# A fused two-stage convolution and attention kernel: VectorE's order within a step, the place of a small matmul on TensorE, and where input statistics stand

## The chip, the cores and the metric

The kernel runs on one core of a Trainium2 chip. The metric is the device time of one execution in microseconds (us); lower is better. A time is compared only with times of the same kind of run on the same chip.

## The reference

The input x is 32 images of 64 channels, 28 by 28, float32. Two blocks follow each other, each with a residual.

```python
x = x + relu(sum_over_4_branches(lambda * bn2(bconv3x3(relu(bn1(bconv3x3(tile(gn(x), 4), w1))), w2))) + gn(x))
g = gn(x)                                   # second block
m = resize(masks, 28 x 28)                  # bilinear, one mask per image
mid = g * m
atten = sigmoid(conv7x7([mean_c(mid), max_c(mid), m]))
out = mid * atten
x = x + relu(5 * (instance_norm(out) * in_gamma + in_beta))
```

`gn` is a group norm with 32 groups, that is pairs of channels. `bconv3x3` is a grouped 3x3 convolution of the signs of its input and of its weights. The second convolution has real-valued relu outputs in front of its sign, so that what it really reads is whether each output of the first convolution passes a threshold.

## The kernel before

**Tiles.** A tile t holds two images (2 x 64 channels on 128 partitions, 784 columns); there are 16 tiles, 0 to 15. `X` holds the tiles (later overwritten in place by X1, the result of the first block), `o` the second block's work.

**Steps.** Each engine has its program written out by hand, in order, and waits on semaphores. The main part is a loop over k = 0 to 14, one step per tile (TensorE L1342 to L1365, VectorE L1042 to L1071, ScalarE L733 to L749, GpSimd L540 to L550 with k from 1). A step works on several tiles at once, each at another stage. What one step does, with the names used below:

- TensorE, step k: `conv2(k,0)` (L1181), `conv1(k+1,0)` (L1160), `turn(k-2,0)` (L1232, transposes of the attention input), `conv2(k,1)`, at four of the steps a `group_1` (L1120), then `group_2(k-1)` (L1128: the sum over channel pairs of X1's statistics), `conv1(k+1,1)`, on even k `attention(k-3)` (L1248), `mix(k,0)` and `mix(k,1)` (L1200), `turn(k-2,1)`, `turn(k-2,2)`, `join(k+2)` (L1142).
- VectorE, step k: `split_sums(k,0)` (L867), `stats_x1(k-1)` (L776 and L781, statistics of X1), `reduce_chunks(k-2,0)` (L908, L910: the first channel maxima), `gates(k+1,0)` (L841, L844, L847), `split_sums(k,1)`, `terms1` at four of the steps, `terms2(k-1)` (L812 to L817), `gates(k+1,1)`, `finish_block(k)` (L875), `reduce_chunks(k-2,1)` and `(k-2,2)`, and `stats_x(t)` (L776, L781) for the input tiles that the dictionaries `X_END` and `X_MID` name. `X_MID`'s tiles (9, 12 and 14, at k = 4, 6, 8) stand in front of `finish_block`.
- ScalarE, step k: `round_sums2(k,0)` (L623), `move_back(k,0)` (L630), `round_sums1(k+1,0)` (L615, writes `first`), `last_relu(k-7)` (L675), the same three for the other half, `sigmoid` (L650), `sign_x` (L583), `mean_o` (L662), `normalise2(k-1)` (L642), `square_o` (L669), `pack_signs(k+2)` (L598), `relu_block(k)` (L636).
- GpSimd, iteration k: `add_x(k-1)` (L485), `attend(k-5)` (L480), `scale3(k-6)` (L492 to L498), `last_sum(k-7)` (L521), `power2(k-1)` (L457, L459), `mask_column`, `make_u(k-1)` (L465).
- SyncE issues all the large transfers in order: the inputs, then two stores of the resized masks (L362) which wait for `keep_mask_rows` (L1010), then per step mask rows (L321), attention rows (L327, L335) and outputs (L341).

**What sets the order around the change.** These waits tie the moved pieces to others:

- `gates(t,q)` waits for ScalarE's `first` of that half (`whole1`), and its results go into S, which `conv2(t,...)` reads. Its first instruction reads `first` (int16) and writes `gate0` (float16), both in SBUF: L841. `conv2(k+1,0)` waits for both halves of `gates(k+1,...)`.
- `stats_x1(t)` waits for GpSimd's `add_x(t)`. `group_2(t)` waits for `stats_x1(t)`. `terms2(t)` waits for `group_2(t)`, and `power2(t)`, `normalise2(t)` and `make_u(t)` for it in turn.
- `mix(k,hh)` waits for `split_sums(k,hh)` and for `gates(k+1,0)`. `conv1(k+1,1)` waits for `split_sums(k,0)`.
- `attention(t)` waits for the first maxima of the next tile, since they share a PSUM bank:

```python
pe.wait_ge(pooled, t * 3 + (4 if t < NT - 3 else 3))      # L1239
```

In step k that is `attention(k-3)` and `reduce_chunks(k-2,0)`.

After the loop comes a tail for the last tiles, which the change does not touch.

Of the kernel before, what the change touches and what calls it, by code (L numbers as in the profile page):

```python
# [71 lines left out]
def wait(eng, sem, count):  # L72

    if count > 0:
        eng.wait_ge(sem, count)


def has(t):
    return 0 <= t < NT


def build(nc, x, w1, w2, par, scale1, masks, band_w, cst, out):
# [8 lines left out]
    with ctx:  # L91
# [107 lines left out]
        def sums(name, first_half=0, halves=2):  # L199
            at = LOW + HALF * first_half  # L200
            return big[SLOT[name]][:, at:at + halves * HALF]

        def c1(t, q):

            return "c2_1" if t == 0 and q == 1 else f"c1_{q}"

        def inside(padded, row=0, rows=H):
            at = padded[:, PW + 1 + row * PW:PW + 1 + (row + rows - 1) * PW + W]
            return bass.AP(at.tensor, at.offset, [list(at.ap[0]), [PW, rows], [1, W]])
# [63 lines left out]
        BATCHES = [(0, 1), (1, 2), (2, 4), (4, 6), (6, 9), (9, 12), (12, 16)]  # L273
        BATCH_STEP = {2: 3, 4: 4, 7: 5, 10: 6}

        X_END = {1: (4, 5), 2: (6,), 3: (7, 8), 4: (10,), 5: (11,), 7: (13,), 9: (15,)}
        X_MID = {4: (9,), 6: (12,), 8: (14,)}

        def batch(t):
            return next(n for n, (a, z) in enumerate(BATCHES) if a <= t < z)  # L280
# [20 lines left out]
        def turned_at(t, n):  # L301
            return LAST_BANKS[t][n] if t in LAST_BANKS else small[1 - n % 2]
# [470 lines left out]
        def _(dve):  # L773
            def stats_of(t, n, src):
                for i in range(2):
                    dve.bn_stats(bnst[:, n, t, i, :], src[:, HALF * i:HALF * (i + 1)]).then_inc(stats[n], 1)  # L776
                add_up(t, n)
# [5 lines left out]
            def stats_x(t):  # L783
                if has(t):
                    dve.wait_ge(x_in[t], 16)
                    stats_of(t, 0, X[:, t, :])

            def stats_x1(t):
                if has(t):
                    dve.wait_ge(x1_ready, t + 1)  # L790
                    stats_of(t, 1, X[:, t, :])
# [32 lines left out]
            def terms1(n):  # L824
                dve.wait_ge(group1, n + 1)
                if n >= 3:

                    dve.wait_ge(group2, next(k for k in BATCH_STEP if BATCH_STEP[k] == n))
                group_terms(0, *BATCHES[n], group1_at(n), nm1, ve1, mean1, steps1, n + 1, var1)
# [6 lines left out]
            def gates(t, q):  # L836

                row = TOP if t == 0 else 0
                at = row * W
                dve.wait_ge(whole1, t * 2 + q + 1)  # L840
                dve.tensor_scalar(gate0[:, q, at:HW], first[:, q, at:HW], thr[:, q:q + 1], GATE, ALU.is_gt, ALU.mult)\  # L841
                   .then_inc(gated0, 1)
                ps = sums(c1(t, q))[:, at:HW]
                dve.scalar_tensor_tensor(ps, first[:, q, at:HW], -IMG, ps, ALU.mult, ALU.add).then_inc(parted1, 1)  # L844
                dve.wait_ge(parted1, t * 2 + q + 1)
                wait(dve, conv2_done, t * 2 - 2)
                dve.scalar_tensor_tensor(inside(S2[:, t % 2, q, :], row, H - row),  # L847
                                         ps.rearrange("p (h w) -> p h w", w=W), thr[:, q:q + 1],
                                         gate0[:, q, at:HW].rearrange("p (h w) -> p h w", w=W), ALU.is_gt, ALU.add)\
                   .then_inc(gated, 1)  # L850
# [12 lines left out]
            def split_sums(t, hh):  # L863
                if has(t):
                    dve.wait_ge(rounded2, t * 2 + hh + 1)
                    wait(dve, y_done, (t - 2) * 2 + hh + 1)
                    dve.scalar_tensor_tensor(RD[:, t % 2, hh, 1, :], round2[:, hh, :], BASE, sums(f"c2_{hh}"),  # L867
                                             ALU.subtract, ALU.subtract).then_inc(split, 1)
# [31 lines left out]
            def reduce_chunks(t, n):  # L900
                if not has(t):
                    return
                dve.wait_ge(turned, t * 3 + n + 1)
                wait(dve, att_done, t // 2 - 1)
                j0, nj = 3 * n, min(3, NJ - 3 * n)
                ps = turned_at(t, n)[0:CP, 0:nj * (P + 2)].rearrange("p (j m) -> p j m", m=P + 2)
                dst = [red[:, t // 2 % 2, c, 1 + j0:1 + j0 + nj, 2 * (t % 2):2 * (t % 2) + 2] for c in range(2)]
                dve.tensor_reduce(dst[1], ps[:, :, 0:P].rearrange("p j (i c) -> p j i c", i=2), AX_X, ALU.max)\  # L908
                   .then_inc(maxed, 1)
                dve.tensor_copy(dst[0], ps[:, :, P:P + 2]).then_inc(pooled, 1)  # L910
# [69 lines left out]
            def keep_mask_h():  # L980
                dve.wait_ge(mask_h, 1)
                dve.tensor_copy(mh[:, :, :].rearrange("p b h -> p (b h)"), small[0][:, 0:MB * H])\
                   .then_inc(mask_hs, 1)

            def keep_mask_hw():
                dve.wait_ge(mask_hw, 1)
                ps = small[0][0:CP, 0:MB * NJ].rearrange("p (b j) -> p b j", j=NJ)
                dve.tensor_copy(mhw[:, 1:MB + 1, :], ps).then_inc(mask_hs, 1)
                dve.tensor_copy(mhw[:, 0, :], ps[:, 0, :]).then_inc(mask_hs, 1)
                dve.tensor_copy(mhw[:, MB + 1, :], ps[:, MB - 1, :]).then_inc(mask_hs, 1)  # L990
# [16 lines left out]
            def keep_mask_rows():  # L1007
                dve.wait_ge(mask_turned, 1)
                for g in range(2):
                    dve.tensor_copy(mR[:, g, :], small[0][0:CP, CP * g:CP * (g + 1)]).then_inc(mask_rows, 1)  # L1010
# [31 lines left out]
            for k in range(NT - 1):  # L1042
                split_sums(k, 0)
                if k == 0:
                    stats_x(3)
                stats_x1(k - 1)
                if k == 1:
                    keep_mask_rows()
                reduce_chunks(k - 2, 0)
                if has(k + 1):  # L1050
                    gates(k + 1, 0)
                if k == 0:
                    keep_mask_h()
                split_sums(k, 1)
                if k == 0:
                    terms1(2)
                    keep_mask_hw()
                if k in BATCH_STEP:
                    terms1(BATCH_STEP[k])
                terms2(k - 1)  # L1060
                if has(k + 1):
                    gates(k + 1, 1)
                for t in X_MID.get(k, ()):
                    stats_x(t)
                finish_block(k)
                if k == 0:
                    mix_masks()
                reduce_chunks(k - 2, 1)
                reduce_chunks(k - 2, 2)
                for t in X_END.get(k, ()):  # L1070
                    stats_x(t)  # L1071
# [39 lines left out]
        def _(pe):  # L1111
# [38 lines left out]
            def conv1(t, q):  # L1150
                pe.wait_ge(packed, t + 1)
                if q == 0:
                    wait(pe, y_added, t - 1)
                    wait(pe, gated, 2 * t - 1)
                else:
                    wait(pe, split, 2 * t - 1)
                acc = big[SLOT[c1(t, q)]]
                for s in range(KS):
                    for hh in range(2):
                        mm = pe.matmul(acc[:, LOW + HALF * hh:LOW + HALF * (hh + 1)],  # L1160
                                       w1t[64 * hh:64 * hh + 64, q, s, :],
                                       window(RH * hh, s // 3, s % 3, E[64 * hh:64 * hh + 64, t % 2, :]),
                                       start=(s == 0), stop=(s == KS - 1))
                mm.then_inc(conv1_done, 1)
# [177 lines left out]
            for k in range(NT - 1):  # L1342
                conv2(k, 0)
                conv1(k + 1, 0)
                if k == 0:
                    resize_mask()
                    group_1(2)
                if k == 1:
                    turn_mask()
                turn(k - 2, 0)  # L1350
                conv2(k, 1)
                if k == 1:
                    pe.wait_ge(mask_rows, 2)
                if k in BATCH_STEP:
                    group_1(BATCH_STEP[k])
                group_2(k - 1)
                conv1(k + 1, 1)
                if k == 0:
                    resize_mask_w()
                attention(k - 3)  # L1360
                for hh in range(2):
                    mix(k, hh)
                turn(k - 2, 1)
                turn(k - 2, 2)
                join(k + 2)  # L1365
# [97 lines left out]
```

## Time and profile before

| what | value |
|---|---|
| median of 3 runs | 243.91 us (243.69 to 244.25) |
| profiled execution, its own time | 244.12 us |
| its span | 242.2 us |
| mean granted TensorE clock | 0.973 |
| TensorE matmul busy | 212.1 us, 88% |
| VectorE busy | 213.1 us, 88% |
| ScalarE busy | 182.8 us, 75% |
| GpSimd busy | 158.8 us, 66% |

The span runs from the first to the last instruction of the profiled execution; 1.9 us of the execution's own time lie outside it. Start times in the rows are microseconds from the start of the span. In the timeline a line gives start, duration, engine, source line, operation, output and inputs, shapes, how many instructions were merged, and in brackets the idle time of that engine in front of it with what ended it.

### The profile page before, as it was taken

What the parts mean: (1) busy time and instruction counts of PE and PEld (TensorE: products, weight loads), DVE (VectorE), ACT (ScalarE), POOL (GpSimd) and SP (SyncE); (2) the same over time, 40 slices, a digit from 0 to 9 for tenths busy, and PEclk for the clock granted to TensorE, in tenths of its full rate; (3) what the DMA queues carried; (4) which work ended last, traced back from release to release, by engine and by line L of the source; (5) the groups of instructions that cost most, each with busy time, mean ns of one, the idle gap of its engine ahead of it and who ended that gap; (6) DMA issues with size and microseconds to landing.
All of it is one profiled execution on the core that took longest, in us unless ns stands there. A gap on an engine that the chain in (4) does not pass through costs nothing.

```text
span 242.2 us, 7335 instructions
## 1 busy us (share of the span) xinstructions
PE 212.1 (88%) x2834; PEld 134.2 (55%) x2834; DVE 213.1 (88%) x520; ACT 182.8 (75%) x265; POOL 158.8 (66%) x207
## 2 busy tenths in 40 slices
PE   7789988889999889999899989998999999788800
PEld 3356554555666556665556656655565656457600
DVE  4899899799999999998999899979796979989691
ACT  3973566657696779798889989898999995860592
POOL 4548431609060755749897778897878787797883
PEclk9999999999999999999999999999999999999955
DMA  6999801510111340234121712081208120713345
GB/s 212 371 284 390 346 9 43 136 45 20 49 35 38 98 106 0 69 97 108 70 69 52 218 69 66 29 244 71 69 17 254 69 69 17 250 73 96 108 168 231
DMA packets 12122, 28.85 MB, mean 119 GB/s; under 512 B 2246, under 2 KB 3655, under 8 KB 12087
## 3 DMA queue, kind: packets, MB, share of 16 engines
q1 hardware_dynamic: 11941, 28.37, 36.4%
q8 instruction: 23, 0.38, 0.6%
q14 instruction: 12, 0.10, 0.1%
q10 hardware_dynamic: 146, 0.01, 0.0%
HBM read 21.76 MB, written 6.61 MB: 117 GB/s over the span
## 4 chain that ended last, share of the span: by engine, by line
PE 37%; DVE 31%; POOL 10%; DMA 8%; issue 8%; ACT 4%; SPq 1%; DVEq 0%; POOLq 0%; ACTq 0%
PE big L1181 10%; PE big L1160 10%; DVE bnst L776 6%; PE big L1200 5%; PE small L1232 5%; DVE big L844 4%; POOL X L485 4%; DVE RD L867 4%; DMA o<-in_w 2%; POOL o L465 2%; DMA att_b<-attention_rows 2%; PE small L1248 2%; DVE S L847 2%; DVE gate L841 2%; DVE acc L875 2%
## 5 line engine op out<-in xcount | busy, mean ns | idle before, releaser
L1181 PE MATMUL big<-S,w2t 64*64 64x392 f16 x1152 | 55.3, 332 | 2.9 <-DVE S L847 2.8
L1160 PE MATMUL big<-E,w1t 64*128 64x392 f16 x576 | 54.5, 331 | 1.6 <-DVE w1t L959 0.9
L1181 PEld LDWEIGHTS big<-S,w2t 64*64 64x64 f16 x1152 | 30.8, 106 | 22.6 <-DVE S L847 7.4
L623 ACT ACTIVATE round<-big 128x784 f16<-128x784 f32 x32 | 26.1, 816 | 18.1 <-PE big L1181 17.8
L1200 PE MATMUL big<-RD,wa 128*64 128x392 f16 x384 | 35.1, 331 | 4.8 <-issue 4.8
L1160 PEld LDWEIGHTS big<-E,w1t 64*128 64x128 f16 x576 | 25.8, 94 | 23.7 <-ACT E L598 3.2
L867 DVE SCALAR_TENSOR_TENSOR RD<-round,big 128x784 f16<-128x784 f16 x32 | 30.7, 959 | 8.2 <-ACT round L623 7.9
L465 POOL TENSOR_TENSOR o<-o,mask_b 128x784 f32<-128x784 f32 x15 | 27.8, 1856 | 13.9 <-ACT o L642 10.9
L776 DVE BATCH_NORM_STATS2 bnst<-X 128x6 f32<-128x392 f32 x62 | 31.9, 556 | 3.9 <-POOL X L485 3.6
L485 POOL TENSOR_TENSOR X<-X,acc 128x784 f32<-128x784 f32 x15 | 27.7, 1849 | 10.3 <-ACT acc L636 10.1
L847 DVE SCALAR_TENSOR_TENSOR S<-big,thr,gate 128x784 f16<-128x784 f32 (+1 forms) x32 | 32.3, 1010 | 1.1
L457 POOL TENSOR_TENSOR r<-ve,mhalf 128x1 f32<-128x1 f32 x16 | 10.4, 650 | 33.0 <-DVE ve L817 32.8
L1232 PE MATMUL small<-cs,o 128*112 128x130 f32 x204 | 30.2, 288 | 1.9 <-DVE ve L817 1.4
L1200 PEld LDWEIGHTS big<-RD,wa 128*64 128x64 bf16 x384 | 22.7, 110 | 15.1 <-issue 7.9
L844 DVE SCALAR_TENSOR_TENSOR big<-first,big 128x784 f32<-128x784 int16 (+1 forms) x32 | 30.2, 945 | 0.0
L1232 PEld LDWEIGHTS small<-cs,o 128*112 128x112 f32 x204 | 24.1, 177 | 11.0 <-issue 7.4
L480 POOL TENSOR_TENSOR o<-o,att_b 128x784 f32<-128x784 f32 x14 | 25.9, 1851 | 3.7 <-DMA att_b<-attention_rows 3.7
L615 ACT ACTIVATE first<-big 128x784 int16<-128x784 f32 x30 | 24.5, 817 | 4.9 <-PE big L1160 4.9
L630 ACT ACTIVATE RD<-round 128x784 f16<-128x784 f16 x32 | 27.4, 857 | 1.0
L521 POOL TENSOR_TENSOR o<-o,X 128x784 f32<-128x784 f32 x12 | 22.1, 1844 | 0.0
L642 ACT ACTIVATE o<-X,nmr,r 128x784 f32<-128x784 f32 x15 | 15.6, 1037 | 7.0 <-POOL nmr L459 7.0
L908 DVE TENSOR_REDUCE red<-small 112x6 f32<-112x384 f32 (+1 forms) x44 | 19.4, 446 | 0.5 <-PE small L1232 0.5
(161 smaller groups left out, 326.3 us busy)
## 6 DMA issues: line engine op xcount, KB each, us to landing
X<-in_x SPq DMA_DIRECT2D x16, 392.0 KB, 13.1
mask_b<-mask_rows SPq DMA_DIRECT2D x32, 196.0 KB, 4.0
out<-o SPq DMA_DIRECT2D x15, 392.0 KB, 2.7
att_b<-attention_rows SPq DMA_DIRECT2D x28, 196.0 KB, 3.9
o<-in_w SPq DMA_DIRECT2D x3, 576.0 KB, 6.8
o<-in_masks SPq DMA_DIRECT2D x1, 512.0 KB, 9.7
band<-in_band SPq DMA_DIRECT2D x1, 441.0 KB, 10.1
cs<-in_cst SPq DMA_DIRECT2D x1, 399.0 KB, 8.8
```

Of the source, the lines that this page charges most:

```text
L465: pool.tensor_tensor(o[:, t, :], o[:, t, :], mask_b[:, t % 2, :], ALU.mult).then_inc(u_ready, 1)
L485: pool.tensor_tensor(X[:, t, :], X[:, t, :], acc0[:, t % 2, :], ALU.add).then_inc(x1_ready, 1)
L623: act.activation(round2[:, hh, :], sums(f"c2_{hh}"), ACT.Copy, bias=BASE - MID).then_inc(rounded2, 1)
L630: act.activation(RD[:, t % 2, hh, 0, :], round2[:, hh, :], ACT.Copy, bias=-BASE).then_inc(whole2, 1)
L776: dve.bn_stats(bnst[:, n, t, i, :], src[:, HALF * i:HALF * (i + 1)]).then_inc(stats[n], 1)
L844: dve.scalar_tensor_tensor(ps, first[:, q, at:HW], -IMG, ps, ALU.mult, ALU.add).then_inc(parted1, 1)
L847: dve.scalar_tensor_tensor(inside(S2[:, t % 2, q, :], row, H - row), ps.rearrange("p (h w) -> p h w", w=W), thr[:, q:q + 1], gate0[:, q, a ...
L867: dve.scalar_tensor_tensor(RD[:, t % 2, hh, 1, :], round2[:, hh, :], BASE, sums(f"c2_{hh}"), ALU.subtract, ALU.subtract).then_inc(split, 1)
L1160: mm = pe.matmul(acc[:, LOW + HALF * hh:LOW + HALF * (hh + 1)], w1t[64 * hh:64 * hh + 64, q, s, :], window(RH * hh, s // 3, s % 3, E[64 * ...
L1181: mm = pe.matmul(acc[64 * q:64 * q + 64, LOW + HALF * r:LOW + HALF * (r + 1)], w2t[64 * r:64 * r + 64, s, 64 * q:64 * q + 64], window(RH * ...
L1200: mm = pe.matmul(big[SLOT["y"]][64 * i:64 * i + 64, at:at + HALF], wa[:, i, r, n, :], RD[:, t % 2, hh, i, HALF * r:HALF * (r + 1)], start= ...
L1232: mm = pe.matmul(turned_at(t, n)[0:CP, at:at + P + 2], o[:, t, CP * j:CP * (j + 1)], turn_w[:, :] if t == LAST else cs[:, K_ID:K_ID + P + ...
```

## The change

On VectorE the step's order becomes `split_sums(k,0)`, `keep_mask_rows` (at k = 1), `gates(k+1,0)`, `stats_x1(k-1)`, `reduce_chunks(k-2,0)`, and then as before. The input statistics of tiles 9, 12 and 14 move from in front of `finish_block` to the end of the same step. On TensorE `conv1(k+1,1)` goes in front of `group_1` and `group_2(k-1)`. No instruction is added or taken away.

```diff
-        X_END = {1: (4, 5), 2: (6,), 3: (7, 8), 4: (10,), 5: (11,), 7: (13,), 9: (15,)}
-        X_MID = {4: (9,), 6: (12,), 8: (14,)}
+        X_END = {1: (4, 5), 2: (6,), 3: (7, 8), 4: (9, 10), 5: (11,), 6: (12,), 7: (13,), 8: (14,), 9: (15,)}
@@ VectorE's loop
                 split_sums(k, 0)
                 if k == 0:
                     stats_x(3)
-                stats_x1(k - 1)
                 if k == 1:
                     keep_mask_rows()
-                reduce_chunks(k - 2, 0)
                 if has(k + 1):
                     gates(k + 1, 0)
+                stats_x1(k - 1)
+                reduce_chunks(k - 2, 0)
                 if k == 0:
                     keep_mask_h()
                 split_sums(k, 1)
@@
                     gates(k + 1, 1)
-                for t in X_MID.get(k, ()):
-                    stats_x(t)
                 finish_block(k)
@@ TensorE's loop
                 if k == 1:
                     pe.wait_ge(mask_rows, 2)
+                conv1(k + 1, 1)
                 if k in BATCH_STEP:
                     group_1(BATCH_STEP[k])
                 group_2(k - 1)
-                conv1(k + 1, 1)
                 if k == 0:
                     resize_mask_w()
```

## Rows read from the trace of the kernel before

**Rows 1.** The page: busy time of each engine, and the chain that ended last, by engine.

```profile
PE 212.1 (88%) x2834; PEld 134.2 (55%) x2834; DVE 213.1 (88%) x520; ACT 182.8 (75%) x265; POOL 158.8 (66%) x207
...
PE 37%; DVE 31%; POOL 10%; DMA 8%; issue 8%; ACT 4%; SPq 1%; DVEq 0%; POOLq 0%; ACTq 0%
```

**Rows 2.** Busy time by stretch: stretch, length, PE, PEld, DVE, ACT, POOL, clock, DMA.

```profile
132.00:205.00 73.00, 70.83 (x1014) 44.99 (x1005) 63.96 (x143) 64.66 (x93) 59.91 (x70) 1.00 0.33 102
```

**Rows 3.** Timeline, step 9 and the beginning of step 10, all engines.

```profile
134.47 1.84 POOL L485 TENSOR_TENSOR X<-X,acc 128x784 f32<-128x784 f32 x1 [1.21 <-ACT acc L636]
...
135.14 0.97 DVE L867 SCALAR_TENSOR_TENSOR RD<-round,big 128x784 f16<-128x784 f16 x1 [0.92 <-ACT round L623]
...
135.90 0.81 ACT L615 ACTIVATE first<-big 128x784 int16<-128x784 f32 x1
...
136.28 1.85 POOL L480 TENSOR_TENSOR o<-o,att_b 128x784 f32<-128x784 f32 x1
136.35 1.04 DVE L776 BATCH_NORM_STATS2 bnst<-X 128x6 f32<-128x392 f32 x2 [0.24 <-POOL X L485]
...
138.04 0.42 DVE L841 TENSOR_SCALAR gate<-first,thr 128x784 f16<-128x784 int16 x1
138.10 0.41 POOL L492 TENSOR_SCALAR ve<-o_square 128x1 f32<-128x1 f32 x1
138.37 0.97 DVE L844 SCALAR_TENSOR_TENSOR big<-first,big 128x784 f32<-128x784 int16 x1
...
139.74 0.82 ACT L615 ACTIVATE first<-big 128x784 int16<-128x784 f32 x1 [0.26 <-PE big L1160]
...
140.33 0.96 DVE L867 SCALAR_TENSOR_TENSOR RD<-round,big 128x784 f16<-128x784 f16 x1
...
141.52 0.22 DVE L817 SCALAR_TENSOR_TENSOR ve<-dm,veps 128x1 f32<-128x1 f32 x1
...
143.00 1.04 DVE L847 SCALAR_TENSOR_TENSOR S<-big,thr,gate 128x784 f16<-128x784 f32 x1
...
144.09 1.33 PEld L1181 LDWEIGHTS big<-S,w2t 64*64 64x64 f16 x36 [0.39 <-DVE S L847]
...
147.04 0.97 DVE L867 SCALAR_TENSOR_TENSOR RD<-round,big 128x784 f16<-128x784 f16 x1
```

**Rows 4.** Timeline, step 10: its attention, and the start of step 11.

```profile
152.05 1.08 PE L1248 MATMUL small<-band,red 112*28 112x56 f32 x36
...
156.61 1.72 PE L1181 MATMUL big<-S,w2t 64*64 64x392 f16 x36
...
159.70 0.97 DVE L867 SCALAR_TENSOR_TENSOR RD<-round,big 128x784 f16<-128x784 f16 x1 [1.41 <-ACT round L623]
```

**Rows 5.** Timeline, conv2(k,0) of k = 5 and of k = 15, first and last of 11.

```profile
81.41 1.72 PE L1181 MATMUL big<-S,w2t 64*64 64x392 f16 x36 [0.47 <-DVE S L847]
...
204.81 1.38 PE L1181 MATMUL big<-S,w2t 64*64 64x392 f16 x28
```

**Rows 6.** Timeline, an early VectorE operation alone and beside GpSimd's add_x.

```profile
31.91 0.19 DVE L1000 TENSOR_SCALAR mlo<-mhw 112x56 f32<-112x56 f32 x1
...
32.18 1.88 POOL L485 TENSOR_TENSOR X<-X,acc 128x784 f32<-128x784 f32 x1 [3.25 <-ACT acc L636]
32.40 1.72 DVE L1000 TENSOR_SCALAR mlo<-mhw 112x56 f32<-112x56 f32 x1
```

**Rows 7.** Timeline, tile 0's short gates; then line L841 over the whole span.

```profile
16.83 0.30 DVE L841 TENSOR_SCALAR gate<-first,thr 128x364 f16<-128x364 int16 x1
17.05 0.53 DVE L844 SCALAR_TENSOR_TENSOR big<-first,big 128x364 f32<-128x364 int16 x1
...
L841 DVE TENSOR_SCALAR gate<-first,thr x32: 304/416/422, 16.8 to 202.4; 128x784 f16<-128x784 int16 x30, 128x364 f16<-128x364 int16 x2
```

**Rows 8.** Timeline, step 1's mask rows and step 2's statistics of X1.

```profile
36.48 0.40 DVE L1010 COPY mR<-small 112x112 f32<-112x112 f32 x2
...
48.36 1.04 DVE L776 BATCH_NORM_STATS2 bnst<-X 128x6 f32<-128x392 f32 x2 [1.46 <-POOL X L485]
```

## The prediction

> **What bounds the kernel now.** I read the page first, then the busy time by stretch, then the timeline of two steps in the middle. No engine alone is the bound: TensorE and VectorE are both busy 88% of the span, and the chain that ended last goes 37% through TensorE and 31% through VectorE [rows 1]. In the late steps TensorE is busy 70.8 of 73 us at the full clock, VectorE 64.0, ScalarE 64.7 [rows 2]. Ten steps, k = 5 to 14, take 204.81 - 81.41 = 123.4 us [rows 5], 12.3 each.
>
> What closes the loop of a step is seen in [rows 3], counted from the start of split_sums(k,0), called Z here (135.14). ScalarE's round ends and lets it go; behind it ScalarE needs until Z+1.6 (135.90 + 0.81 = 136.71) for `first` of the next tile. GpSimd's add_x starts at Z-0.67 and ends at Z+1.2; attend follows at once and runs from Z+1.14 to Z+2.99 (136.28 + 1.85 = 138.13). VectorE's statistics of X1 start when add_x ends, at Z+1.21, after a wait of 0.24. The first gates start at Z+2.90 (138.04), the second split at Z+5.19 (140.33), terms2 gives its variance at Z+6.4, the second gates end at Z+8.90 (144.04), and conv2 of the next step starts at 144.09, held by them. From terms2 the chain also runs through GpSimd's power and ScalarE's normalise, square, pack and relu to the next Z: 147.04, 11.90 after the last one. On even steps attention starts at Z+5.01 (152.05 against 147.04); from there TensorE is full to the next conv2(k,0), 4.56 later, and ScalarE's queue behind the sigmoid gives the next Z 7.65 after attention's start (159.70) [rows 3, 4].
>
> **The change, part by part.** No instruction is new, so the sum is made of waits.
>
> *Gates in front of X1's statistics, the main term.* In the new order the first gates could start when `first` is there, at Z+1.6. At that moment GpSimd is inside attend, from Z+1.14 to Z+2.99, in every step from k = 5 on. The question is whether L841 can run beside it. [Rows 6] show a case: L1000, a tensor_scalar with input and output in SBUF, takes 0.19 us alone, and 1.72 us when it is issued at 32.40 while add_x runs from 32.18 to 34.06; it ends at 34.12, 0.06 after add_x. So it stood still until GpSimd was done. L841 is of the same kind. It is also fast: with 364 columns the next instruction follows 0.22 us later, with 784 columns 0.33 us later (138.04 to 138.37, the next gate instruction), so 420 more columns cost 0.11 us, near four a cycle of a pass that costs L844 0.44 us for the same 420. None of its 32 instances ever took more than 0.422 us [rows 7], but all of them start where no long GpSimd operation is running: in [rows 3] it starts 0.09 us before attend's end, because the statistics and the maxima in front of it happen to take as long as attend. And GpSimd's one-element L492 beside it takes 0.41 us [rows 3]. So I bound the price of the overlap from both sides: 0 (it runs, Z+1.6) and the rest of attend, 1.35 us (Z+2.95 or so). I take the second, since the one overlap in this trace cost all of it.
>
> The Trainium skill, "SBUF — State Buffer", section "SBUF: two separate sides", says that VectorE in its two-port modes and GpSimd share one pair of ports, and that the one that starts first holds it for its whole instruction while the other blocks. By that rule the gates wait for attend; the trace agrees with it in the 1.72 us of [rows 6], and the other end of the bound would be the sum without it.
>
> Then, on odd steps: gates start at Z+2.95, their three instructions hold VectorE 2.29 us (138.04 to 140.33), statistics and maxima 1.69 (136.35 to 138.04), so the second split starts at Z+6.93 instead of Z+5.19. Everything behind hangs on it (terms2, the second gates, conv2, the next Z): +1.74. Five such steps, k = 5, 7, 9, 11, 13: +8.7.
>
> On even steps attention must wait for the maxima, which now come last. They end at Z+2.95+2.29+1.19+0.57 = Z+7.0 (1.19 for the statistics, 0.57 for the reduction with its copy), so attention starts at Z+7.05 instead of Z+5.01: +2.04, and up to +2.2 where no group_1 stood in front of it. Five such steps: +10.5. Together +19.2.
>
> *The small sum behind conv1(k+1,1).* TensorE comes to it earlier by 0.35 us and the wait of some 0.3 in front of it, and conv1 with them. That is gain only if the statistics are there when TensorE arrives. They are ready at Z+2.95+2.29+1.28 = Z+6.5, and TensorE gets there at about Z+4.2 (conv1(k+1,1) ends at about 139.7 now, when ScalarE's 139.74 can start [rows 3], and comes 0.35 or more earlier), so it stands 2 us and more. The earlier conv1 gives an earlier `first`, whose reader, the second gates, is not the last to come. Cost and gain 0; the cover of that is the statistics' wait already counted. If the gates did not have to wait, this wait would still be near 1.
>
> *The early steps.* At k = 1 the mask rows are kept before the statistics, whose 1.1 us stand in front of 36.48 now. SyncE's two stores, the mask loads behind them, and make_u(0) follow, so that add_x(1), for which VectorE waits 1.46 us at 48.36 [rows 8], ends 1.0 earlier. The DMAs keep their order on SyncE's queue and pass nothing. Until k = 4 GpSimd has no attend, and VectorE is late enough that `first` is there: the gates cost no wait. Stepped through with the durations above, conv2(3,0) comes 1.2 us earlier, steps 3 and 4 give 0.8 back through the maxima in front of attention(1), and conv2(5,0) starts 0.35 earlier. The bounds here are -1.5 and +0.5.
>
> *Input statistics at the end of the step.* Same number, three steps. finish_block(k) and with it relu and add_x come 1.2 us earlier; at k = 4 and 8 that removes ScalarE's wait, some 0.4 us each, which at k = 8 lies behind attention anyway. At k = 5, where VectorE has two tiles to do, the step also grows less, by 1.1 instead of 1.74. Together -0.6.
>
> *Sum.* 19.2 - 0.35 - 0.6 = +18.2 us at conv2(15,0). The tail starts from attention(11) and the last add_x as before, both moved with it, so I add nothing. The profiled execution took 244.12 us, so 262.3; the median of the runs shown lies 0.2 below that execution, so **262.0 us**.
>
> **The rivals.**
>
> *A, the gates run beside attend.* For it: L1000 is float32 and L841 int16 to float16, and only one case is in the trace. Against: the kind of operands is the same. Then the gates start at Z+1.6: +0.4 on odd steps, and attention at Z+5.7, +0.7 to +0.9 on even ones. 5 x 0.4 + 5 x 0.8 = 6.0, less the early 0.35 and about 0.9 for the earlier relu in steps 5, 7 and 9: +4.8, **248.7 us**. TensorE's stop at group_2 would be seen here too.
>
> *B, the phases slip.* The longer steps move GpSimd against VectorE. Where attend waits for its attention rows or make_u ends late, the gates come first, hold the ports for 0.33 us, and only then attend starts. If half of the ten steps fall so, half of 13.4 is saved: **255 us**.
>
> *C, the other sign.* The mask rows' gain of 1.2 us stays, and the order helps: the 0.24 us wait for add_x is gone, mix(k,0) no longer waits for the gates (it does in [rows 3]'s step until 138.04 + 2.38 = 140.42), and conv1 is not behind the sum, 0.35 us in each of five odd steps. That gives -1.2 - 1.75, **241 us**. It decides in this case only if the statistics end before TensorE comes to the sum, that is if the gates start 0.5 us or more in front of Z+1.6. ScalarE's two instructions between Z and `first` (1.6 us in [rows 3]) speak against it: they are the same in the new order.
>
> *D, nothing moves.* The early gain and the waits cancel within 0.2%, 0.5 us, which is about what a measurement of this kernel can tell from no change: **243.9 us**.
>
> **How the numbers follow.** The forecast 0.65, B 0.12, A 0.13, C 0.06, D 0.04. All of the first three are slower: 0.90. Faster 0.06, same 0.04. The forecast's own range is 257 to 266: if GpSimd's next small operation also goes ahead of the gates, 0.3 us a step or 3 in all are added; and if the price holds only in the last eight steps, 4 are taken off. To take in B and half of A the whole range goes down to 248.0. Above 266 I leave nothing but the tail of the forecast.
>
> **What would show it.** In the changed kernel's timeline at k = 5 and later, L841 of the first half should be issued about Z+1.6 and last some 1.7 us instead of 0.42, ending within 0.1 us of attend's end; the median of L841 should split in two groups of 16. The wait of TensorE for VectorE's aggregate (L781) at L1128 should grow from 0.3 to about 2 us a step, and attention should start about Z+7. Steps should last 13.6 (odd) and 14.6 us (even). L1010 should come near 35.4, and conv2(3,0) 1.2 us earlier than before. I am wrong in the main term if L841 stays at 0.42 us beside attend (A), wrong in the phases if it is long in some steps only (B), and wrong in the sign if TensorE's wait at L1128 does not grow (C).

## The result, and the profile after

The changed kernel takes **263.89 us** (median of 4 runs, 262.98 to 265.10), the kernel before 244.08 (4 runs, 243.69 to 244.31): ratio 1.082, 95% interval 1.076 to 1.087. The forecast was 262.0 in a range of 248 to 266. The profiled execution took 264.64 us, its span is 262.9.

The page of the changed kernel, its busy time, TensorE's granted clock in 40 slices and the chain that ended last; the line numbers are 3 lower than before on TensorE, 1 lower on the others.

```profile
PE 220.5 (84%) x2834; PEld 135.5 (52%) x2834; DVE 225.0 (86%) x520; ACT 182.1 (69%) x265; POOL 158.0 (60%) x207
...
PEclk9999999999999999799999999899979999979955
...
DVE 42%; PE 22%; issue 18%; ACT 12%; DMA 2%; POOL 2%; SPq 0%; ACTq 0%; DVEq 0%; POOLq 0%
```

Against [rows 1] the chain has left TensorE for VectorE. VectorE is 12 us busier with the same 520 instructions: one that stands still after its issue counts as busy, not as idle. The clock line has four dips in front of its end, which the kernel before did not have there. By lines, 11.2 of the 12 us are in one place, L840, whose median is all but unchanged (0.420 us for 0.416) while its longest went from 0.422 us [rows 7] to 1.614. From the source line's view:

```profile
L840 DVE TENSOR_SCALAR gate<-first,thr x32: 307/420/1614, 17.0 to 220.8; 128x784 f16<-128x784 int16 x30, 128x364 f16<-128x364 int16 x2
```

This is step 8 of the changed kernel in the timeline, whose counterpart is [rows 3]; Z, the start of split_sums(k,0), is at 126.80.

```profile
126.80 0.97 DVE L866 SCALAR_TENSOR_TENSOR RD<-round,big 128x784 f16<-128x784 f16 x1
127.57 0.81 ACT L614 ACTIVATE first<-big 128x784 int16<-128x784 f32 x1
127.95 1.85 POOL L479 TENSOR_TENSOR o<-o,att_b 128x784 f32<-128x784 f32 x1
...
128.41 1.61 DVE L840 TENSOR_SCALAR gate<-first,thr 128x784 f16<-128x784 int16 x1 [0.63 <-ACT first L614]
...
133.22 0.38 PE L1125 MATMUL small<-mv,cs 128*128 128x2 f32 x2 [1.88 <-DVE mv L780]
...
133.58 0.96 DVE L866 SCALAR_TENSOR_TENSOR RD<-round,big 128x784 f16<-128x784 f16 x1
133.71 1.08 PE L1245 MATMUL small<-band,red 112*28 112x56 f32 x36
...
138.23 1.72 PE L1178 MATMUL big<-S,w2t 64*64 64x392 f16 x36
```

The gates are issued at Z+1.61, while attend runs from Z+1.15 to Z+3.00, and end at Z+3.22, 0.22 us behind it. The second split starts at Z+6.78 (5.19 before), attention at Z+6.91 (Z+4.79 in the same step before), and TensorE stands 1.88 us in front of the sum. From k = 6 to 14 all nine first gates are like this, 1.46 to 1.61 us long; at k = 5, where attend starts at Z+0.05 and the gates at Z+0.85, 1.27. Over the run TensorE's wait for that line grew from 0.8 to 18.7 us, its weight loads' from 4.3 to 23.6. From the view of the waits, each line with the total in us, how often, and the longest:

```profile
PEld small L1125 <- DVE mv L780: 23.6, 15, 2.3
...
PE small L1125 <- DVE mv L780: 18.7, 14, 1.9
```

conv2(3,0) starts at 55.65 instead of 56.70, conv2(5,0) at 81.06 instead of 81.41, conv2(15,0) at 223.79 instead of 204.81. So the loss is in the ten steps from 5 on, which took 142.7 us instead of 123.4, +19.3, and 1.7 more in the tail.

### The profile page after: what moved, and what is told of

Read it like the earlier page. It is cut to its first block, busy times and chain, and to the rows that moved or that the text cites. A ratio compares the mean times of both kernels' runs of the same rounds, so it can differ in the third digit from the quotient of the medians.

```text
span 262.9 us, 7334 instructions
## 1 busy us (share of the span) xinstructions
PE 220.5 (84%) x2834; PEld 135.5 (52%) x2834; DVE 225.0 (86%) x520; ACT 182.1 (69%) x265; POOL 158.0 (60%) x207
## 4 chain that ended last, share of the span: by engine, by line
DVE 42%; PE 22%; issue 18%; ACT 12%; DMA 2%; POOL 2%; SPq 0%; ACTq 0%; DVEq 0%; POOLq 0%
DVE bnst L775 9%; DVE big L843 7%; DVE S L846 7%; PE big L1197 5%; PE big L1178 4%; PE big L1157 4%; DVE RD L866 4%; ACT first L614 3%; PE small L1245 3%; PE small L1229 2%; DMA o<-in_w 2%; ACT round L622 2%; DVE gate L840 2%; DVE red L907 1%; ACT unread L668 1%
## 5 line engine op out<-in xcount | busy, mean ns | idle before, releaser
L1197 PE MATMUL big<-RD,wa 128*64 128x392 f16 x384 | 40.0, 361 | 0.0
L484 POOL TENSOR_TENSOR X<-X,acc 128x784 f32<-128x784 f32 x15 | 27.8, 1851 | 11.4 <-ACT acc L635 9.3
L1229 PE MATMUL small<-cs,o 128*112 128x130 f32 x204 | 31.2, 294 | 2.0 <-DVE ve L816 2.0
L1229 PEld LDWEIGHTS small<-cs,o 128*112 128x112 f32 x204 | 25.1, 182 | 11.3 <-issue 8.5
L840 DVE TENSOR_SCALAR gate<-first,thr 128x784 f16<-128x784 int16 (+1 forms) x32 | 24.3, 761 | 6.5 <-ACT first L614 6.5
L1197 PEld LDWEIGHTS big<-RD,wa 128*64 128x64 bf16 x384 | 21.4, 119 | 13.0 <-DVE RD L866 1.8
```

Source lines behind the costliest of these rows:

```text
L1197: mm = pe.matmul(big[SLOT["y"]][64 * i:64 * i + 64, at:at + HALF], wa[:, i, r, n, :], RD[:, t % 2, hh, i, HALF * r:HALF * (r + 1)], start= ...
L1229: mm = pe.matmul(turned_at(t, n)[0:CP, at:at + P + 2], o[:, t, CP * j:CP * (j + 1)], turn_w[:, :] if t == LAST else cs[:, K_ID:K_ID + P + ...
```

## The experiments

All are compared with the kernel before on their own chip. Its median there was 246.6 us for e1 to e4, 245.1 for e5 to e8 and 246.1 for e9 to e11, with more scatter than in the first comparison (243.4 to 248.9). In seven of the eleven profiles of the experiments TensorE's granted clock fell once or more in the first 50 us, which neither profile of the first comparison shows. Differences under 1 us are therefore read from the steps in the traces, not from the times.

**e1 and e2: the same swap on GpSimd, in the changed kernel and in the one before.** In both, attend comes later, and the small operations of scale3 earlier. At k = 5 there is no scale3 yet, and attend stays where it was.

```diff
                 add_x(k - 1)
-                attend(k - 5)
                 scale3(k - 6)
+                attend(k - 5)
                 last_sum(k - 7)
```

> The changed kernel, with GpSimd's scale3(k-6) in front of attend(k-5), so that at 1.6 us behind the first split only small operations run there and attend starts near 2.8. Ports theory (the first gates stood still because attend held the ports): the gate instruction is back at about 0.42 us, the second split starts at +5.6 instead of +6.77, attention at +5.7 instead of +6.91, and the time falls from 264 to about 249 to 251 us. Order theory (the cost comes from the order itself, gates waiting for first and statistics, sum and maxima behind them): the time stays within 2 us of 264.

Measured: 250.76 us (249.60 to 253.01), ratio to the kernel before 1.022 (1.014 to 1.029). The order of VectorE and TensorE is that of the changed kernel, and the time is 13 us below its 263.9, though in another comparison. In the traces the ten steps from 5 on take 128.7 us for its 142.7. Timeline of step 8, Z = 124.60:

```profile
124.60 0.97 DVE L866 SCALAR_TENSOR_TENSOR RD<-round,big 128x784 f16<-128x784 f16 x1
...
126.20 0.43 DVE L840 TENSOR_SCALAR gate<-first,thr 128x784 f16<-128x784 int16 x1 [0.63 <-ACT first L614]
...
127.34 1.85 POOL L479 TENSOR_TENSOR o<-o,att_b 128x784 f32<-128x784 f32 x1
...
130.18 0.96 DVE L866 SCALAR_TENSOR_TENSOR RD<-round,big 128x784 f16<-128x784 f16 x1
```

The gates take 0.43 us at the same Z+1.60, and the second split is at Z+5.58, as the ports theory said. All nine from k = 6 on are short; at k = 5, where attend has not moved, they take 1.25 us as in the changed kernel.

> The kernel before, with the same swap on GpSimd. Now attend runs from about +2.8 to +4.6, where the first gates start in the old order at +2.9. Ports theory: the gates, in their old place, take up to 1.9 us instead of 0.42 and the kernel before becomes 12 to 20 us slower, about 256 to 264, without any change on VectorE or TensorE. Order theory: within 2 us of 244.

Measured: 257.17 us (256.42 to 258.27), ratio 1.047 (1.040 to 1.054), so 10.6 us slower, a little under the expected 12 to 20, inside the 256 to 264. Nothing changed on VectorE. Timeline of step 9, Z = 141.48:

```profile
141.48 0.97 DVE L867 SCALAR_TENSOR_TENSOR RD<-round,big 128x784 f16<-128x784 f16 x1 [0.92 <-ACT round L623]
...
144.12 1.84 POOL L480 TENSOR_TENSOR o<-o,att_b 128x784 f32<-128x784 f32 x1
...
144.39 1.80 DVE L841 TENSOR_SCALAR gate<-first,thr 128x784 f16<-128x784 int16 x1
145.93 1.96 POOL L521 TENSOR_TENSOR o<-o,X 128x784 f32<-128x784 f32 x1
146.11 0.96 DVE L844 SCALAR_TENSOR_TENSOR big<-first,big 128x784 f32<-128x784 int16 x1
```

The gates in their old place now meet attend and take 1.80 us; so do all nine from k = 6 on, 1.80 to 1.82. They end 0.23 us behind attend, while last_sum, the next long GpSimd operation, has already started. So the order theory falls: the kernel before owes its time to the moment at which its gates came, just when attend ended.

**e5: the gates in another form, with one of their inputs in PSUM.** The changed lines, shortened; this kernel computes other gates and so another result, and serves for its timing alone.

```diff
+                if q == 0 and t > 5:
+                    dve.scalar_tensor_tensor(gate0[...], first[...], thr[:, q:q + 1], ps, ALU.is_gt, ALU.is_gt)
+                else:
                     dve.tensor_scalar(gate0[...], first[...], thr[:, q:q + 1], GATE, ALU.is_gt, ALU.mult)
```

> The changed kernel; the first gates' L840 from tile 6 on is another operation of the same size, with one input in SBUF and one in PSUM (it compares with the convolution's sum instead of multiplying by 1024, so the gates of those tiles are other values). Such an operation takes a cycle per column, near 0.9 us instead of 0.42. Ports theory: it does not wait for attend and is the cheaper one here, about 0.95 us instead of 1.61, the second split starts at +6.1 instead of +6.77, and the time is 4 to 7 us lower, 257 to 260. Rival, any operation of VectorE on SBUF waits for attend: 1.6 us and more, the time 264 or up to 268.

Measured: 257.24 us (254.99 to 257.91), ratio 1.050 (1.043 to 1.057). Timeline of step 8, Z = 124.24:

```profile
125.38 1.86 POOL L479 TENSOR_TENSOR o<-o,att_b 128x784 f32<-128x784 f32 x1
125.84 1.03 DVE L842 SCALAR_TENSOR_TENSOR gate<-first,thr,big 128x784 f16<-128x784 int16 x1 [0.63 <-ACT first L614]
126.79 0.97 DVE L847 SCALAR_TENSOR_TENSOR big<-first,big 128x784 f32<-128x784 int16 x1
...
130.43 0.96 DVE L870 SCALAR_TENSOR_TENSOR RD<-round,big 128x784 f16<-128x784 f16 x1
```

This operation, issued 0.46 us into attend, runs through in 1.03 us. The one that alone takes 0.42 took 1.61 there. The second split is at Z+6.19, between e1 and the changed kernel. The wait belongs to the form of the operation, not to VectorE beside GpSimd as such. Input in SBUF alone is not what makes the difference either: the statistics of X1, which read SBUF and write SBUF, take 1.04 us for two beside attend [rows 3], and in the changed kernel none of the 62 takes more than 0.57. Whether the kind of operation or the operand in PSUM made e5's gates free was not separated.

**e6: the new order on VectorE alone, TensorE's sum where it was.** The order in short:

```diff
                 split_sums(k, 0)
-                stats_x1(k - 1)
                 if k == 1:
                     keep_mask_rows()
-                reduce_chunks(k - 2, 0)
-                if has(k + 1):
-                    gates(k + 1, 0)
+                gates(k + 1, 0)
+                stats_x1(k - 1)
+                reduce_chunks(k - 2, 0)
```

> The kernel before with the new order on VectorE in all steps, but TensorE as before, the sum still in front of conv1(k+1,1). Theory that moving the sum is what keeps the change from costing more: conv1 now waits for the statistics until +6.6, the second gates come some 1.3 us later than in the changed kernel and attention 1.7, so about 275 to 282 us. Rival, the place of the sum makes no difference: 262 to 265.

Measured in a single execution: 295.17 us, beyond both. The direction was right, the size was not: 31 us above the changed kernel where 11 to 18 were expected. Timeline of step 7:

```profile
131.79 0.38 PE L1130 MATMUL small<-mv,cs 128*128 128x2 f32 x2 [3.22 <-DVE mv L781]
...
132.11 2.73 PE L1162 MATMUL big<-E,w1t 64*128 64x392 f16 x18
...
134.77 2.76 PE L1202 MATMUL big<-RD,wa 128*64 128x392 f16 x24
...
135.73 0.42 DVE L841 TENSOR_SCALAR gate<-first,thr 128x784 f16<-128x784 int16 x1 [1.58 <-ACT first L615]
```

TensorE stands 3.2 us, conv1 waits with it, and then takes 2.73 us instead of 1.70, since the clock has fallen. The second gates wait 1.6 us for it. The mean granted clock was 0.901; how much of the 31 us is the clock and how much the waits was not tried. Putting the sum behind conv1 was the part of the change that kept the rest from costing this.

**e3, e9 and e10: what TensorE's stand costs besides.**

```diff
                 conv1(k + 1, 1)
+                if k > 4:
+                    for _ in range(10):
+                        pe.matmul(small[0][:, 0:HALF], warm[:, 0:P], warm[:, :], start=True, stop=True)
                 if k in BATCH_STEP:
```

> The changed kernel, with ten spare matmuls (1.6 us in all) in front of the group sums from k = 5 on, where TensorE stands 1.5 to 1.9 us. Theory that TensorE's stand is what lets its clock fall three times in the middle of the run (k = 6, 10, 12, each some 1.3 us): no 0.5 stretches between 60 and 220 us, steps 6, 10 and 12 shrink from about 16.0 to 14.4, the time is 4 us lower, about 260. Rival, the clock falls for another reason or costs nothing: 264 or, if the matmuls come in the way, more.

Measured: 261.45 us (261.28 to 261.72), ratio 1.064 (1.058 to 1.071), against 1.082 for the changed kernel in its own comparison. The clock stayed at 1.00 from 60 to 225 us and steps 6, 10 and 12 took 14.4 us each, as expected. To have them side by side, both ran again.

> The changed kernel once more, as it is, on the chip of the two runs beside it. Theory that the stand of TensorE lets its clock fall in some even steps: one to four stretches at 0.5 between 60 and 225 us again, in steps where TensorE stands 1.5 us or more, and 262.5 to 265.5 us.

> The changed kernel with the ten spare matmuls, on the same chip. Theory: no stretch at 0.5 between 60 and 225 us, every even step between 13.7 and 14.5 us, and 2 to 4 us less than the changed kernel beside it. Rival, the difference of the first two runs came from two chips: same time as the changed kernel.

Measured: e9, the changed kernel, 263.94 us (262.67 to 265.06, granted clock 0.947 to 0.954); e10 260.87 us (259.76 to 262.35, clock 0.966 to 0.974). No run of the one reaches the other. Busy time by stretch, with the columns of [rows 2], first two stretches of e9, then the same two of e10:

```profile
130.00:165.00 35.00, 29.76 (x390) 18.35 (x388) 30.98 (x69) 24.68 (x38) 22.65 (x28) 0.90 0.21 71
200.00:225.00 25.00, 21.54 (x264) 13.29 (x254) 20.57 (x39) 15.60 (x22) 16.81 (x21) 0.86 0.17 51
```
```profile
130.00:165.00 35.00, 34.35 (x447) 21.22 (x442) 32.07 (x71) 26.52 (x41) 23.66 (x30) 1.00 0.22 71
200.00:225.00 25.00, 24.46 (x328) 14.86 (x324) 22.61 (x49) 17.15 (x25) 17.48 (x21) 1.00 0.23 71
```

With the stand filled the clock stays at 1.00, and all steps from 6 to 13 of e10 last 13.5 to 14.4 us. In the changed kernel it falls to half in partly other places each time (steps 6, 10 and 12 in the first profile, 8, 10 and the end of 13 with the beginning of 14 in e9), and a step that has the whole fall lasts 15.8 to 16.1. This is how it looks in the changed kernel, the timeline of the two mixes of step 10, disturbed, and of step 8:

```profile
162.65 3.66 PE L1197 MATMUL big<-RD,wa 128*64 128x392 f16 x24
...
134.72 2.18 PE L1197 MATMUL big<-RD,wa 128*64 128x392 f16 x24
```

**e4, e7, e8 and e11: the change's other parts, e4 with the gates' move in the early steps alone.**

```diff
 e4, k < 3 alone:        keep_mask_rows, gates(k+1,0), stats_x1(k-1), reduce_chunks(k-2,0); TensorE as before
 e7:                     conv1(k + 1, 1) in front of group_1 and group_2, nothing else
 e8, e11:                e7, X_MID emptied into X_END, and
+                if k == 1:
+                    keep_mask_rows()
                 stats_x1(k - 1)
-                if k == 1:
-                    keep_mask_rows()
```

> The kernel before, with the new order of VectorE (mask rows first, gates in front of X1's statistics and maxima) at k = 1 and 2 alone; TensorE as before. Theory that the mask rows' earlier way to GpSimd is worth 1.05 us at conv2(3,0) and stays until the end: 242.9 against 243.9. Rival, it is absorbed by the later steps: no difference.

Measured: 249.05 us (245.63 to 252.00), ratio 1.007 (1.002 to 1.013): neither, it is a little slower. The gates stand in front of the statistics at k = 1, the sum waits for them until Z+5.0, and conv1(2,1) stands behind the sum. In the profile, that of the slowest execution, the second gates of step 1 end at Z+11.4 instead of 8.4, part of it a fall of the clock in that step. So the likely reading is that TensorE's old order takes what the mask rows bring; how much of it is the clock this profile can't tell.

> The kernel before, with TensorE's part of the change alone: conv1(k+1,1) in front of the sums. The statistics come early in the old order, so TensorE loses the 0.3 us it stands in front of the sum, in the even steps where it is full; the odd steps are held by VectorE. Theory: 1 to 2 us faster, 242 to 243 on a chip where the kernel before takes 244. Rival: terms2 comes later by conv1's 1.65 us and with it normalise and the next step: same or 1 us slower.

Measured: 244.23 us (242.97 to 246.82), ratio 0.995 (0.991 to 0.999). The expected mechanism did not show: attention starts at Z+4.78 as before, and all steps from 5 to 13 are within 0.02 us of the kernel before. The 0.3 us in front of the sum was not time that TensorE could have used. In the one profile, step 2 is 1.0 us shorter, because the mask rows' transfers took 7.2 us from copy to use instead of 8.2, which varies between executions (7.2 to 8.6 in the eleven profiles in which GpSimd waits for them). The interval lies just under 1, but no step shows a gain that the edit would explain, so whether half a per cent is real stays open.

> The kernel before, with everything of the change but the gates' place: mask rows first at k = 1, input statistics at the end of the step, the sum behind conv1. Theory: mask rows 1.0, statistics 0.4 each at k = 6 and 8, sum 1 to 2: 2.5 to 4 us faster than the kernel before, near 240.5. Rival, each is absorbed by the steps behind it: within 0.5 us of before.

Measured: 243.16 us (241.92 to 245.66), ratio 0.989 (0.984 to 0.994).

> The kernel before with mask rows first, input statistics last and the sum behind conv1, the gates in their old place, a second time. Theory: the gain of some 2 us over the kernel before is there again, ratio 0.985 to 0.995. Rival, it was scatter of the clock in the first 60 us: interval across 1.

Measured: 243.52 us (241.87 to 246.47), ratio 0.991 (0.986 to 0.996). This version beats both kernels, by 2 to 2.5 us on the kernel before. By the steps in e11: step 2 is 1.4 us shorter (12.46 for 13.85), step 5 0.24, steps 7 and 9 0.47 and 0.44, and the other steps from 1 on are equal; step 0 is 2.6 us longer, with a fall of the clock in it, which is why this profile's span is no shorter than before. In step 2 the mask rows are copied 1.2 us earlier; the other 0.2 is the transfers' scatter. The last three gains go with the input statistics at the end, which e7 leaves in place without such a gain. They let finish_block and ScalarE's relu go earlier: 1.15 us together, where the expectation had 0.4 each at two steps. Its chain goes through TensorE again:

```profile
PE 67%; DVE 22%; issue 4%; DMA 3%; ACT 3%; POOL 1%; SPq 0%; DVEq 0%
```

## Why the prediction was right, and where it was off

**The main term's mechanism was right.** L840 is long ten times, once in each step from k = 5 on, as forecast. e1 and e2 show that it is attend that it waits for, and e5 that the form of the operation makes it do so. No run shows the ports themselves, only this wait. The median did not split as I had written, since 22 of 32 stay short.

**Its size on even steps was right.** Without a fall of the clock they grew by 2.12 and 2.11 us (k = 8 and 14) where the working had 2.04 to 2.2, attention starting at Z+6.91 for 7.05.

**Its size on odd steps was too large.** The term was +1.74 each, 8.7 in all, less 0.64 for k = 5 under the input statistics; measured by the starts of conv2 they grew by 0.33, 0.60, 1.15, 1.01 and 1.08 us, 4.2 in all. Four things are seen in it; what each is worth by itself was not tried. The gates' next instruction follows at Z+3.14, 0.14 us before the Z+3.28 of the working (second split at Z+6.77 for 6.93), so the next Z comes 13.5 us later for 13.64. At k = 5 the gates were issued at Z+0.85 and got through by Z+2.12, since attend had started with Z, so the second split moved by 0.65 us only. At k = 7 and 9 the kernel before lost 0.45 us through the input statistics in front of finish_block, of which I counted only a part. And behind a step with a fallen clock Z follows conv2 at 2.63 us instead of 3.0, which gives a part of that step's loss back.

**A term was missing.** The working had TensorE stand 2 us a step in front of the sum, which came (1.6 to 1.9), and priced it at nothing beyond the wait. The clock fell to half three times in these steps and again in the tail: steps 6, 10 and 12 grew by 3.8, 3.5 and 3.6 us instead of 2.1. e10 against e9 puts the whole of it at 3.1 us by the medians, 4.3 by the two profiles. The tail's +1.7, for which the sum had nothing, is the clock too: the same kernel's profile in e9 has no fall there (0.84 for 0.77, from conv2(15,0) to the end) and a tail of 36.9 us, against 39.1 in the first profile and 37.4 in the kernel before.

**So the sum was nearer than its terms, and that is luck**: 18.2 us forecast at conv2(15,0), 19.0 measured, with odd steps 4 too dear and the clock's 4 left out. With the clock held up, in e10, the ten steps took 139.4 us, +16.0, where the working had +18.6. The early steps came near: conv2(5,0) 0.35 us earlier, as worked out, and conv2(3,0) 1.05 for 1.2. But the mask rows' transfers alone scatter by as much as this gain, so one profile can't confirm it to a tenth.

**The rivals.** A, no wait: e1 is what it would have been, near enough, 250.8 us for the 248.7 worked out, since there the gates do not meet attend from k = 6 on. It also gives the share of the order itself: over the ten steps it takes 5.3 us more than the kernel before, and the changed kernel 14.0 more than e1, for the wait and the clock that fell with it. B, slipping phases: it did not happen. The gates never came in front of attend; at k = 5 the phase slipped the other way, with attend 1.1 us earlier against Z, and elsewhere Z and attend kept their distance, since both hang on the same relu. C, the gain: its first part, the mask rows, is there in e8; its second, conv1 freed from the sum, is not (e7). D, nothing moves, fell with the ratio of 1.082.

## What to carry to other kernels

An operation's place in an engine's queue has a second meaning when it shares a resource with another engine: look at what the neighbour runs at the new moment, not only at what the operation waits for. The fast VectorE form was worth its speed only where no long GpSimd operation was running (0.42 us alone, 1.61 beside attend). Beside attend a slower form was done earlier (1.03 us in e5), and among the versions with early gates the best was the one that moved GpSimd's long operation behind them (e1); leaving the gates in their old place was better still (e8 and e11). And a wait put in front of TensorE can cost more than its length, when the clock falls with it.

## What the runs showed of the hardware

- The wait counts as busy time: VectorE's busy share hid it, and only the spread of one line's durations (0.42 and 1.61 us) gave it away.
- It goes both ways. GpSimd's one-element L492 takes 0.41 us beside the gates [rows 3] and 0.19 in e1 and e2, where it runs without them.
- The waiting VectorE operation did not have to wait for two GpSimd operations that stand back to back: in e2 it ended 0.23 us behind the first, and the second then took 1.96 to 1.97 us instead of 1.84, all eight times.
- The clock fell to half (0.5 of full speed in the records, that is 1.2 GHz) in steps in which TensorE never stood longer than 1.9 us at a time, though 1.1 to 1.9 once in every step, and not once between 60 and 225 us when ten spare matmuls filled the stand. The Trainium skill, "TensorE: Matmul & The Clock Gate", section "Part 1: The HAM clock gate (the "warmup" mystery)", says of the mechanism that activity releases a throttle that is there by default. The trace agrees with that much: more work kept the clock up and made the run 3 us shorter.
- Standing alone does not decide it. In e2 TensorE stood 2.0 to 2.2 us in every second step and 0.7 to 0.9 in the others, in front of the mixes (L1200), and the clock stayed at 1.00 from 60 to 225 us. What sets the one apart from the other stays open. From e2's view of the waits:

```profile
PE big L1200 <- issue: 14.9, 13, 2.2
```
